# A third bank for the scores of the last eight slots, and three high parts rounded by GpSimd, in an attention block

## The chip, the cores and the metric

The kernel runs on one core of a Trainium2 chip. The metric is device time in microseconds of one execution. TensorE (PE) multiplies into PSUM, VectorE (DVE), ScalarE (ACT) and GpSimd (POOL) work on what it leaves, and SyncE (SP) issues most transfers. GpSimd is used here on SBUF operands alone; the scores lie in PSUM.

## The reference

x has the shape (4, 256, 32, 32): four images, 256 channels, 1024 positions. The reference is a residual self-attention block with four heads of 64 channels:

```
x_n = group_norm(x, 32 groups) * gn_w + gn_b
q, k, v = conv1x1(x_n, wq, bq), conv1x1(x_n, wk, bk), conv1x1(x_n, wv, bv)
q, k, v = to_heads(q), to_heads(k), to_heads(v)          # (b, 4, 1024, 64)
attn = softmax(einsum('bhqd,bhkd->bhqk', q, k) * 64 ** -0.5, axis=-1)
out = einsum('bhqk,bhkd->bhqd', attn, v)
return x + conv1x1(out, wp, bp)
```

## The kernel before, in words

Every fp32 product is made of three fp16 products: each operand is split into a high part (rounded to fp16) and a low part (the difference to fp32, rounded to fp16), and high x high, high x low and low x high are summed in PSUM.

The attention is cut into 128 slots, `TOTAL`, numbered G = 0 to 127, 32 for each image. Four slots make a unit: one head, one half (512) of the queries, and all 1024 keys in four steps of 256. A slot consists of these steps.

- `scores(G)` on TensorE (L718): four products, two for each of two 128-key blocks, into a pair of banks of 1024 fp32 columns. There are two such pairs, `st[0]` and `st[1]`, used by even and odd slots. The second product of each block subtracts a shift, an upper bound made from row maxima, so that the exponential stays in range.
- `exponent(G)` on ScalarE (L954): the exponential of the scores once rounded to fp16 into `p_hi` (L964) and once in fp32 (L969). Even slots write the fp32 copy over the scores in PSUM ("in place"), odd slots write it into one of three SBUF buffers `p32`.
- `p_low(G)`: the difference of the two. Even slots, and the last five slots (`TAIL`), do it on VectorE in two halves (L1086); the other odd slots do it on GpSimd in one piece (L1328).
- `weigh(G)` on TensorE (L747): 24 small products of `p_hi` and `p_lo` with the values, four slots after the scores; the last slots catch up by the table `LAST_WEIGHED`, so that slot 124 weighs slots 120 and 121, and slot 125 weighs 122 and 123.
- After each unit VectorE divides by the denominators, `normalise` (L1089), and the first weighing of the next unit waits for that (L755).

The shift of a unit comes from products of 128 queries with 512 keys of both heads of a pair (`pair_of_maxima`, L686), which VectorE reduces (`row_max`, L1046). Eight such products belong to a pair of units; the last pair is V = 15, for slots 120 to 127. Up to V = 14 two of them are made in every second slot, one in the scores bank `st[1]` that is free just then, and one in the banks `mx`. The eight of V = 15 are made one by one in slots 110 to 117, all in `mx`, so that each waits for the reduction of the one before (L700). After the last, `row_shift` writes the shift, and a transfer puts it into a row of `q_max`, for which slot 120 waits.

The output projection `job("y", ...)` of an image is made in two halves of three products each. For the first 512 positions of the last image, the first halves of the two channel blocks stand in slots 122 and 123 (L805 to L808), in the bank `gen` and in the first bank of `mx`; the second halves follow after slot 127 (L902, L903), ahead of the weighing of slots 126 and 127.

The order of the work is written out by hand for each engine, in loops over the slots. On VectorE a slot runs `p_low(G - 1)` first, then the reductions that `reduced_at(G)` lists, then `normalise` (L1137). On GpSimd slot 117 splits an attention output into high and low part and adds a bias to the residual (`split_output`, `add_bias`), slot 118 does `p_low(117)`, slot 119 the second `add_bias`, slots 120 and 122 do `p_low(119)` and `p_low(121)`, slot 125 splits another output (L1331).

Of the kernel before, what the change touches and what calls it, by code (L numbers as in the profile page):

```python
# [8 lines left out]
ACT = mybir.ActivationFunctionType  # L9
# [3 lines left out]
def attention_block(nc, x, gn_w, gn_b, wq, bq, wk, bk, wv, bv, wp, bp, out):  # L13
    B, C, IH, IW = x.shape
# [7 lines left out]
    HALF = HW // 2  # L22
    QT = HALF // P
    UNITS = HEADS * 2
    SPU = 4
    CPS = NK // SPU
    SLOTS = UNITS * SPU
    TOTAL = B * SLOTS
# [6 lines left out]
    PR = 8  # L35
# [40 lines left out]
    MAX_AFTER = ((), ((0, 0), (0, 1)), (), ((0, 6), (0, 7)), ((1, 0), (1, 1)), ((1, 2), (1, 3)))  # L76
    TAIL = 5

    LAST_WEIGHED = {4: (8, 7), 3: (6, 5), 2: (4,), 1: (3,)}
# [3 lines left out]
    with ctx:  # L83
# [3 lines left out]
        def sem(name):  # L87
            return ctx.enter_context(nc.semaphore(name))
# [73 lines left out]
        first_banks = [st[0][:, 0:512], st[0][:, 512:1024], st[1][:, 0:512], st[1][:, 512:1024], gen, st[1][:, 0:512]]  # L162
        tail_banks = [st[0][:, 0:512], st[0][:, 512:1024], st[1][:, 0:512], st[1][:, 512:1024]]
        last_banks = [gen, mxb[0]]
        row_bank = st[1][:, 512:1024]
# [60 lines left out]
        s_plo_dve = sem("s_plo_dve")  # L226
        s_plo_pool = sem("s_plo_pool")
        s_pv = sem("s_pv")
        s_o32 = sem("s_o32")
# [14 lines left out]
        def wait(eng, s, v):  # L244
            if v > 0:
                eng.wait_ge(s, v)
# [41 lines left out]
        def pair_maxima(G):  # L288

            V, m = divmod(G + PAIR_AHEAD, 2 * SPU)  # L290
            if G in FIRST_PAIRS:
                return [("two", SINGLES // 2, m) for m in FIRST_PAIRS[G]]
            if V == LAST_PAIR:
                return [("two", V, m)]
            if m % 2 or not SINGLES // 2 < V < LAST_PAIR:
                return []
            return [("two", V, m), ("two", V, m + 1)]

        def in_scores_bank(V, m):

            return m in FIRST_IN_SCORES if V == SINGLES // 2 else V < LAST_PAIR and m % 2 == 0

        def maxima_at(G):
            return pair_maxima(G) + single_maxima(G)
# [13 lines left out]
        def one_slot_later(kind, n, m):  # L318

            return kind == "two" and SINGLES // 2 < n < LAST_PAIR and m % 2 == 1  # L320

        def reduced_at(G):

            return [item for item in maxima_at(G) if not one_slot_later(*item)] + \
                   [item for item in pair_maxima(G - 1) if one_slot_later(*item)]

# [65 lines left out]
        def in_place(G):  # L392

            return G % 2 == 0 and G > 0

        def wait_p_lo(eng, G, c=CPS - 1):

            n = sum(lo_on_dve(m) == lo_on_dve(G) for m in range(G))
            wait(eng, *((s_plo_dve, CPS * n + c + 1) if lo_on_dve(G) else (s_plo_pool, n + 1)))
# [23 lines left out]
        def v_rows(tile, i, j):  # L423
            return tile[:, i, 4 * j:4 * j + 4, :, 0:D].rearrange("p c h d -> p (c h) d")

        def p_full(G):

            tile = st[G % 2][:, :] if in_place(G) else p32[:, G // 2 % PB if G else PB - 1, :]
            return tile.rearrange("p (c n) -> p c n", n=HALF)
# [167 lines left out]
        def _(pe):  # L597
# [120 lines left out]
            def scores(G):  # L718
# [12 lines left out]
                if s == 0 and U >= SINGLES and U % 4 == 0:  # L731
                    wait(pe, s_dup_k, 16 * 6 * (U // 4 + 1))
                    wait(pe, s_dup_q[0], 16 * 6 * (U // 4 + 1))
                if G > 1 and not in_place(G - 2):
                    wait(pe, s_exp, G - 1)
                if pair_in_bank(G) is not None:
                    wait(pe, s_mx_free, pair_in_bank(G) + 1)
                for c in range(CPS):
                    if G > 1 and in_place(G - 2):
                        wait_p_lo(pe, G - 2, c)  # L740
                    k = slice((CPS * s + c) * P, (CPS * s + c + 1) * P)
                    dst = st[G % 2][:, c * HALF:(c + 1) * HALF]
                    nc.tensor.matmul(dst, k_both[:, head, k], q_twice[:, head, q], start=True, stop=False)  # L743
                    last = nc.tensor.matmul(dst, k_one[:, head, k], q_max[:, head, q], start=False, stop=True)  # L744
# [40 lines left out]
            def slot(G):  # L785
# [17 lines left out]
                if todo:  # L803
                    job(*todo, only=0 if todo[0] in LONG else None)
                if G in (TOTAL - 6, TOTAL - 5):  # L805
                    i = G - TOTAL + 6
                    wait(pe, s_mx_free, len(in_order))
                    job("y", i, 0, B - 1, last_banks[i], only=0)  # L808

# [92 lines left out]
            job("y", 0, 0, B - 1, last_banks[0], only=1)  # L902
            job("y", 1, 0, B - 1, last_banks[1], only=1)  # L903
            weigh(TOTAL - 2)
# [12 lines left out]
        def _(act):  # L917
# [36 lines left out]
            def exponent(G):  # L954
                scores = st[G % 2][:, :].rearrange("p (c n) -> p c n", n=HALF)
                wait(act, s_st, G + 1)
                wait(act, s_pv, G + 1 - PR)
                if G == TOTAL - 1:
# [4 lines left out]
                    return  # L963
                nc.scalar.activation(p_hi[:, G % PR, :, :], scores, ACT.Exp, scale=SM_SCALE / M_SCALE)  # L964
                if G == 2 * PB - 1:
# [295 lines left out]
        def _(pool):  # L1261
# [64 lines left out]
            def p_low(G):  # L1326
                wait(pool, s_exp, G + 1)
                nc.gpsimd.tensor_tensor(p_lo[:, G % PR, :, :], p_full(G), p_hi[:, G % PR, :, :], ALU.subtract)\  # L1328
                  .then_inc(s_plo_pool, 1)
# [82 lines left out]
```

## Time and profile before

| what | value |
|---|---|
| median of 3 runs | 367.43 us (366.38 to 367.86) |
| the profiled execution | 366.56 us |
| its span, first to last instruction | 364.8 us |
| mean granted TensorE clock | 0.998 |
| TensorE busy | 348.0 us, 95% |
| ScalarE busy | 303.1 us, 83% |
| VectorE, GpSimd busy | 284.0 and 284.2 us, 78% each |

The span holds a prologue of about 16 us, then the 128 slots up to about 358 us, then the last projection and the stores. Slot 110 starts on TensorE at 315.84 us of the span, slot 120 at 338.36 us, slot 127 at 353.23 us. A row of the timeline gives the start, the duration, engine, line and operation, the tile written and the tiles read, their shapes, and in brackets the idle time of the engine before it with what ended it. The weight load of a product (PEld) has its own row.

### The profile page before, as it was taken

The numbers are of one execution on the slowest core, as the hardware profiler recorded it, in microseconds if no ns is written. First come the engines' busy times: TensorE is split into PE (matmuls) and PEld (weight loads), VectorE is DVE, ScalarE is ACT, GpSimd is POOL, SyncE is SP. The second block draws the span as 40 slices with busy tenths as digits, with TensorE's granted clock in tenths as the row PEclk, the third lists the DMA queues.
The fourth block names the chain that finished last, engine by engine and source line by source line (L and its number), as shares of the span: only waits on it lengthen the run. The fifth ranks groups of instructions, "written<-read, shape, count | busy, mean of one in ns | idle before, by whom it ended". The sixth has DMA issues, their size and how long they took to land.

```text
span 364.8 us, 11244 instructions
## 1 busy us (share of the span) xinstructions
PE 348.0 (95%) x4577; PEld 208.6 (57%) x4577; DVE 284.0 (78%) x447; ACT 303.1 (83%) x362; POOL 284.2 (78%) x258
## 2 busy tenths in 40 slices
PE   0899999999999999999999999999999999999996
PEld 0544565655656556655666556565656556655564
DVE  5788899878887787778887777777877787787474
ACT  1748879898877999989878999998889888888982
POOL 5066888699788997998778997998879797967722
PEclk9999999999999999999999999999999999999999
DMA  6055141213743341143553241031552441070113
GB/s 212 19 146 144 45 97 38 30 62 103 135 142 74 80 98 43 24 112 116 124 154 66 60 106 64 10 80 43 117 164 53 94 85 65 2 202 3 31 31 118
DMA packets 38587, 30.92 MB, mean 85 GB/s; under 512 B 23676, under 2 KB 31368, under 8 KB 38536
## 3 DMA queue, kind: packets, MB, share of 16 engines
q1 hardware_dynamic: 37792, 29.15, 32.6%
q10 hardware_dynamic: 744, 1.06, 0.8%
q8 instruction: 37, 0.61, 0.7%
q14 instruction: 14, 0.11, 0.1%
HBM read 9.44 MB, written 4.19 MB: 37 GB/s over the span
## 4 chain that ended last, share of the span: by engine, by line
PE 85%; DVE 8%; ACT 2%; issue 2%; DMA 1%; DVEq 1%; ACTq 0%
PE gen L617 19%; PE st L743 14%; PE st L744 14%; PE pv L766 9%; PE pv L769 8%; PE pv L768 7%; PE st L709 5%; PE mx L709 3%; DVE mx L1053 3%; DVE p_lo L1086 2%; ACT st L969 1%; DVE mx L1049 1%; PE st L617 1%; PE mx L824 1%; DMA xin<-in_x_dram 1%
## 5 line engine op out<-in xcount | busy, mean ns | idle before, releaser
L964 ACT ACTIVATE p_hi<-st 128x1024 f16<-128x1024 f32 x127 | 130.7, 1029 | 40.2 <-PE st L744 38.8
L1328 POOL TENSOR_TENSOR p_lo<-p,p_hi 128x1024 f16<-128x1024 f32 x62 | 132.3, 2133 | 10.4 <-ACT p L969 10.4
L766 PEld LDWEIGHTS pv<-v_hi,p_hi 128*128 128x128 f16 x1024 | 93.4, 97 | 26.7 <-issue 15.0
L766 PE MATMUL pv<-v_hi,p_hi 128*128 128x65 f16 x1024 | 106.4, 195 | 0.3 <-DVE o L1094 0.2
L768 PE MATMUL pv<-v_lo,p_hi 128*128 128x64 f16 x1024 | 105.9, 193 | 0.0
L769 PE MATMUL pv<-v_hi,p_lo 128*128 128x65 f16 x1024 | 105.7, 194 | 0.0
L1086 DVE TENSOR_TENSOR p_lo<-st,p_hi 128x512 f16<-128x512 f32 x126 | 80.8, 683 | 30.0 <-ACT st L969 29.7
L743 PE MATMUL st<-q_twice,k_both 128*128 128x512 f16 x256 | 97.0, 379 | 1.6 <-DVE p_lo L1086 1.2
L768 PEld LDWEIGHTS pv<-v_lo,p_hi 128*128 128x128 f16 x1024 | 93.8, 98 | 6.2
L744 PE MATMUL st<-q_max,k_one 65*128 65x512 f16 x256 | 97.3, 380 | 0.0
L769 PEld LDWEIGHTS pv<-v_hi,p_lo 128*128 128x128 f16 x1024 | 93.9, 97 | 0.0
L1053 DVE TENSOR_REDUCE mx<-st 128x2 f32<-128x1024 f32 x52 | 63.7, 1225 | 25.3 <-PE st L709 25.2
L1053 DVE TENSOR_REDUCE mx<-mx 128x2 f32<-128x1024 f32 x60 | 73.0, 1217 | 1.6 <-PE mx L709 1.6
L969 ACT ACTIVATE st<-st 128x1024 f32<-128x1024 f32 x63 | 65.5, 1040 | 0.0
L969 ACT ACTIVATE p<-st 128x1024 f32<-128x1024 f32 x64 | 65.2, 1018 | 0.0
L743 PEld LDWEIGHTS st<-q_twice,k_both 128*128 128x128 f16 x256 | 25.4, 99 | 26.3 <-issue 7.6
L744 PEld LDWEIGHTS st<-q_max,k_one 65*128 65x128 f16 x256 | 25.0, 97 | 18.4
L459 POOL TENSOR_TENSOR st_lo_k<-e_k,st_hi_k 128x512 f16<-128x512 f32 x16 | 18.5, 1156 | 11.6 <-ACT e_k L939 9.5
L1049 DVE TENSOR_REDUCE mx<-mx 128x1 f32<-128x512 f32 x32 | 20.9, 684 | 4.5 <-PE mx L824 3.0
L1307 POOL TENSOR_TENSOR y<-y,xres 128x512 f32<-128x512 f32 x14 | 17.7, 1270 | 7.6 <-ACT y L948 7.6
L1299 POOL CAST v_hi<-e_v 128x512 f16<-128x512 f32 x16 | 9.8, 614 | 17.0 <-ACT e_v L943 17.0
L617 PE MATMUL gen<-w_hi_v,z_hi 128*128 128x128 f16 x128 | 23.1, 219 | 0.0
(200 smaller groups left out, 558.4 us busy)
## 6 DMA issues: line engine op xcount, KB each, us to landing
q_twice<-st_hi_q SPq DMA_DIRECT2D x64, 64.0 KB, 2.1
xres<-in_x_dram SPq DMA_DIRECT2D x4, 1024.0 KB, 5.2
out_dram<-y SPq DMA_DIRECT2D x13, 256.0 KB, 2.3
xin<-in_x_dram SPq DMA_DIRECT2D x6, 512.0 KB, 4.6
k_both<-st_hi_k SPq DMA_DIRECT2D x16, 128.0 KB, 2.3
k_one<-st_hi_k SPq DMA_DIRECT2D x16, 128.0 KB, 2.6
q_max<-st_lo_q SPq DMA_DIRECT2D x32, 64.0 KB, 2.1
k_both<-st_lo_k SPq DMA_DIRECT2D x16, 128.0 KB, 2.3
```

The lines of the kernel that those rows point to most:

```text
L617: last = nc.tensor.matmul(dst, a, c, start=first and t == 0 and n == 0, stop=t == CT - 1 and n == 2, skip_group_check=True)
L709: last = nc.tensor.matmul(bank[:, h * HALF:(h + 1) * HALF], queries, keys, start=True, stop=True)
L743: nc.tensor.matmul(dst, k_both[:, head, k], q_twice[:, head, q], start=True, stop=False)
L744: last = nc.tensor.matmul(dst, k_one[:, head, k], q_max[:, head, q], start=False, stop=True)
L766: nc.tensor.matmul(pv_v[:, q, :], hi, vh, start=k == 0 and q == 0, stop=False, skip_group_check=True)
L768: nc.tensor.matmul(pv_v[:, q, 0:D], hi, vl, start=False, stop=False, skip_group_check=True)
L769: last = nc.tensor.matmul(pv_v[:, q, :], lo, vh, start=False, stop=k == NK - 1, skip_group_check=True)
L964: nc.scalar.activation(p_hi[:, G % PR, :, :], scores, ACT.Exp, scale=SM_SCALE / M_SCALE)
L969: nc.scalar.activation(p_full(G), scores, ACT.Exp, scale=SM_SCALE / M_SCALE).then_inc(s_exp, 1)
L1053: last = nc.vector.reduce_max(mx8[:, n % 2, :, tile, part], bank[:, :].rearrange("p (h k) -> p h k", h=2), AX.X)
L1086: nc.vector.tensor_tensor(p_lo[:, G % PR, c, :], p_full(G)[:, c, :], p_hi[:, G % PR, c, :], ALU.subtract).then_inc(s_plo_dve, 1)
L1328: nc.gpsimd.tensor_tensor(p_lo[:, G % PR, :, :], p_full(G), p_hi[:, G % PR, :, :], ALU.subtract)\
```

## The change

- The two products m = 0 and 1 of the last pair V = 15 are both made in slot 110, m = 0 in the scores bank `st[1]` and m = 1 in `mx`; slots 111 to 116 make m = 2 to 7, and slot 117 none. VectorE reduces m = 0 in slot 110 and m = 1 in slot 111, ahead of m = 2.
- From slot 120 (`TRIPLE`) on, the scores rotate over three pairs of banks, `mx`, `st[0]`, `st[1]`, and each slot waits for the user of its bank three slots before, not two. Slot 120 waits for the last reduction.
- In slots 117, 119 and 121 (`ONE_EXP`) ScalarE makes the fp32 exponential alone, and GpSimd rounds it to the high part and then subtracts.
- The projection of the second channel block moves as a whole behind slot 127, into `st[1]`; the two tail banks it met there are named anew.

```
+    ONE_EXP = (TOTAL - 11, TOTAL - 9, TOTAL - 7)
+    TRIPLE = TOTAL - 8
...
-        tail_banks = [st[0][:, 0:512], st[0][:, 512:1024], st[1][:, 0:512], st[1][:, 512:1024]]
-        last_banks = [gen, mxb[0]]
+        tail_banks = [st[0][:, 0:512], st[0][:, 512:1024], st[1][:, 512:1024], mxb[0]]
+        last_banks = [gen, st[1][:, 0:512]]
...
             if V == LAST_PAIR:
-                return [("two", V, m)]
+                return [("two", V, n) for n in ((0, 1) if m == 0 else (m + 1,)) if n < 2 * SPU]
...
-            return m in FIRST_IN_SCORES if V == SINGLES // 2 else V < LAST_PAIR and m % 2 == 0
+            return m in FIRST_IN_SCORES if V == SINGLES // 2 else m == 0 or V < LAST_PAIR and m % 2 == 0
...
-            return kind == "two" and SINGLES // 2 < n < LAST_PAIR and m % 2 == 1
+            return kind == "two" and (SINGLES // 2 < n < LAST_PAIR and m % 2 == 1 or (n, m) == (LAST_PAIR, 1))
...
-            return [item for item in maxima_at(G) if not one_slot_later(*item)] + \
-                   [item for item in pair_maxima(G - 1) if one_slot_later(*item)]
+            return [item for item in pair_maxima(G - 1) if one_slot_later(*item)] + \
+                   [item for item in maxima_at(G) if not one_slot_later(*item)]
...
+        def scores_bank(G):
+            return st[G % 2] if G < TRIPLE else (mx, st[0], st[1])[(G - TRIPLE) % 3]
+
+        def bank_user(G):
+            return G - 2 if G < TRIPLE else G - 3
...
-                if G > 1 and not in_place(G - 2):
-                    wait(pe, s_exp, G - 1)
+                if G == TRIPLE:
+                    wait(pe, s_mx_free, len(in_order))
+                elif G > 1 and not in_place(bank_user(G)):
+                    wait(pe, s_exp, bank_user(G) + 1)
...
-                if G in (TOTAL - 6, TOTAL - 5):
-                    i = G - TOTAL + 6
-                    wait(pe, s_mx_free, len(in_order))
-                    job("y", i, 0, B - 1, last_banks[i], only=0)
+                if G == TOTAL - 6:
+                    job("y", 0, 0, B - 1, last_banks[0], only=0)
...
-            job("y", 1, 0, B - 1, last_banks[1], only=1)
+            job("y", 1, 0, B - 1, last_banks[1])
...
-                nc.scalar.activation(p_hi[:, G % PR, :, :], scores, ACT.Exp, scale=SM_SCALE / M_SCALE)
+                if G not in ONE_EXP:
+                    nc.scalar.activation(p_hi[:, G % PR, :, :], scores, ACT.Exp, scale=SM_SCALE / M_SCALE)
...
                 wait(pool, s_exp, G + 1)
+                if G in ONE_EXP:
+                    wait(pool, s_pv, G + 1 - PR)
+                    nc.gpsimd.tensor_copy(p_hi[:, G % PR, :, :], p_full(G)).then_inc(s_phi_pool, 1)
+                    wait(pool, s_phi_pool, ONE_EXP.index(G) + 1)
```

The next two listings are VectorE's order around slots 109 to 112, before and then of the change. `mx8` holds the row maxima; `mx<-mx8` and `shift` close the pair V = 14; the reductions after that are those of V = 15; `p_lo<-st0` is `p_low` of slots 110 and 112.

```order
L1071 TENSOR_REDUCE mx<-mx8 128x8
L1077 TENSOR_SCALAR shift<-mx 128x8
L1053 TENSOR_REDUCE mx8<-mx 128x2
L1086 TENSOR_TENSOR p_lo<-st0,p_hi 128x512 x2
L1053 TENSOR_REDUCE mx8<-mx 128x2
L1093 RECIPROCAL rden<-pv 128x4
L1094 TENSOR_TENSOR o32<-pv,rden 128x4x64
```

```order
L1081 TENSOR_REDUCE mx<-mx8 128x8
L1087 TENSOR_SCALAR shift<-mx 128x8
L1063 TENSOR_REDUCE mx8<-st1 128x2
L1096 TENSOR_TENSOR p_lo<-st0,p_hi 128x512 x2
L1063 TENSOR_REDUCE mx8<-mx 128x2 x2
L1103 RECIPROCAL rden<-pv 128x4
L1104 TENSOR_TENSOR o32<-pv,rden 128x4x64
```

Before, the reduction ahead of `p_lo` is m = 0 and the one behind it m = 1. Now the one ahead is m = 0 out of `st1`, and m = 1 and m = 2, both in `mx`, stand behind it.

The next two listings are GpSimd's order from slot 117 to slot 125, before and then of the change. `o_hi` and `o_lo` are `split_output`, `xres` is `add_bias`, `p_lo` is `p_low` of slots 117, 119 and 121.

```order
L1316 CAST o_hi<-o32 128x512
L1318 TENSOR_TENSOR o_lo<-o32,o_hi 128x512
L1323 TENSOR_SCALAR xres<-xres,bias_y 128x512
L1328 TENSOR_TENSOR p_lo<-p32,p_hi 128x1024
L1323 TENSOR_SCALAR xres<-xres,bias_y 128x512
L1328 TENSOR_TENSOR p_lo<-p32,p_hi 128x1024 x2
L1316 CAST o_hi<-o32 128x512
L1318 TENSOR_TENSOR o_lo<-o32,o_hi 128x512
```

```order
L1326 CAST o_hi<-o32 128x512
L1328 TENSOR_TENSOR o_lo<-o32,o_hi 128x512
L1333 TENSOR_SCALAR xres<-xres,bias_y 128x512
L1340 CAST p_hi<-p32 128x1024
L1342 TENSOR_TENSOR p_lo<-p32,p_hi 128x1024
L1333 TENSOR_SCALAR xres<-xres,bias_y 128x512
L1340 CAST p_hi<-p32 128x1024
L1342 TENSOR_TENSOR p_lo<-p32,p_hi 128x1024
L1340 CAST p_hi<-p32 128x1024
L1342 TENSOR_TENSOR p_lo<-p32,p_hi 128x1024
L1326 CAST o_hi<-o32 128x512
L1328 TENSOR_TENSOR o_lo<-o32,o_hi 128x512
```

Three casts of 1024 columns have come in ahead of three subtractions; nothing else on GpSimd moves. ScalarE's order loses the three `p_hi` passes of these slots.

## Rows read from the trace of the kernel before

**Rows 1.** The page: busy time by engine; shares of the chain that ended last.

```profile
PE 348.0 (95%) x4577; PEld 208.6 (57%) x4577; DVE 284.0 (78%) x447; ACT 303.1 (83%) x362; POOL 284.2 (78%) x258
...
PE 85%; DVE 8%; ACT 2%; issue 2%; DMA 1%; DVEq 1%; ACTq 0%
```

**Rows 2.** Windows: stretch, length, busy PE, PEld, DVE, ACT, POOL, clock, DMA, GB/s.

```profile
334.00:358.00 24.00, 23.22 (x413) 15.90 (x410) 14.99 (x27) 21.86 (x26) 13.49 (x9) 1.00 0.13 24
```

**Rows 3.** Timeline of PE and PEld: what waited, slots 110 to 122.

```profile
317.06 0.41 PE L709 MATMUL mx<-k_both,q_twice 64*128 64x512 f16 x2 [0.18 <-DVE shift L1077]
...
327.03 0.41 PE L709 MATMUL mx<-k_both,q_twice 64*128 64x512 f16 x2 [0.40 <-DVE mx L1053]
...
338.36 0.38 PE L743 MATMUL st<-q_twice,k_both 128*128 128x512 f16 x1 [0.53 <-DVE p_lo L1086]
...
339.46 0.10 PEld L766 LDWEIGHTS pv<-v_hi,p_hi 128*128 128x128 f16 x1 [0.48 <-DVE o L1094]
...
342.24 0.39 PE L743 MATMUL st<-q_twice,k_both 128*128 128x512 f16 x1 [0.26 <-DVE p_lo L1086]
...
342.83 0.10 PEld L743 LDWEIGHTS st<-q_twice,k_both 128*128 128x128 f16 x1 [0.48 <-DVE p_lo L1086]
```

**Rows 4.** Timeline of slot 111: scores and maximum on PE, then DVE.

```profile
318.81 0.38 PE L743 MATMUL st<-q_twice,k_both 128*128 128x512 f16 x1
...
319.77 0.41 PE L709 MATMUL mx<-k_both,q_twice 64*128 64x512 f16 x2
...
319.05 1.29 DVE L1086 TENSOR_TENSOR p_lo<-st,p_hi 128x512 f16<-128x512 f32 x2 [0.32 <-ACT st L969]
320.26 1.22 DVE L1053 TENSOR_REDUCE mx<-mx 128x2 f32<-128x1024 f32 x1
```

**Rows 5.** Timeline of PE: first score product of slots 117, 118, 119.

```profile
332.45 0.38 PE L743 MATMUL st<-q_twice,k_both 128*128 128x512 f16 x1
...
334.49 0.38 PE L743 MATMUL st<-q_twice,k_both 128*128 128x512 f16 x1
...
336.08 0.38 PE L743 MATMUL st<-q_twice,k_both 128*128 128x512 f16 x1
```

**Rows 6.** Timeline of PE: slot 123's projection half, then slot 124's first score product.

```profile
346.26 0.38 PE L617 MATMUL mx<-oT_hi,w_hi_p 128*128 128x512 f16 x1
...
346.91 0.38 PE L743 MATMUL st<-q_twice,k_both 128*128 128x512 f16 x1
```

**Rows 7.** Timeline of DVE: p_low of slot 118, then the division of its unit.

```profile
337.53 1.29 DVE L1086 TENSOR_TENSOR p_lo<-st,p_hi 128x512 f16<-128x512 f32 x2 [1.31 <-ACT st L969]
...
338.98 0.42 DVE L1094 TENSOR_TENSOR o<-pv,rden 128x256 f32<-128x256 f32 x1
```

**Rows 8.** Timeline of POOL: p_low of 115, 117, 121, second add_bias, last split.

```profile
331.20 2.13 POOL L1328 TENSOR_TENSOR p_lo<-p,p_hi 128x1024 f16<-128x1024 f32 x1 [2.42 <-ACT p L969]
...
336.65 2.14 POOL L1328 TENSOR_TENSOR p_lo<-p,p_hi 128x1024 f16<-128x1024 f32 x1
338.77 1.57 POOL L1323 TENSOR_SCALAR xres<-xres,bias_y 128x512 f32<-128x512 f32 x1
...
343.38 2.13 POOL L1328 TENSOR_TENSOR p_lo<-p,p_hi 128x1024 f16<-128x1024 f32 x1 [0.94 <-ACT p L969]
...
348.08 1.49 POOL L1318 TENSOR_TENSOR o_lo<-o,o_hi 128x512 f16<-128x512 f32 x1
```

**Rows 9.** Groups of POOL by shape: busy us, mean ns of one.

```profile
L1328 POOL TENSOR_TENSOR p_lo<-p,p_hi 128x1024 f16<-128x1024 f32 x62 | 132.3, 2133 | 10.4 <-ACT p L969 10.4
L459 POOL TENSOR_TENSOR st_lo_k<-e_k,st_hi_k 128x512 f16<-128x512 f32 x16 | 18.5, 1156 | 11.6 <-ACT e_k L939 9.5
...
L1316 POOL CAST o_hi<-o 128x512 f16<-128x512 f32 x15 | 9.2, 613 | 1.9 <-DVE o L1094 1.9
```

**Rows 10.** Timeline of DVE: p_low of slots 123 and 125, out of SBUF.

```profile
347.70 2.42 DVE L1086 TENSOR_TENSOR p_lo<-p,p_hi 128x512 f16<-128x512 f32 x2 [0.37 <-ACT p L969]
...
352.33 1.28 DVE L1086 TENSOR_TENSOR p_lo<-p,p_hi 128x512 f16<-128x512 f32 x2
```

More of the change, by code:

```diff
@@ L227, in attention_block @@
         s_plo_pool = sem("s_plo_pool")
+        s_phi_pool = sem("s_phi_pool")
         s_pv = sem("s_pv")
@@ L424, in v_rows @@
             return tile[:, i, 4 * j:4 * j + 4, :, 0:D].rearrange("p c h d -> p (c h) d")
+        def scores_bank(G):
+            return st[G % 2] if G < TRIPLE else (mx, st[0], st[1])[(G - TRIPLE) % 3]
+        def bank_user(G):
+            return G - 2 if G < TRIPLE else G - 3
         def p_full(G):
-            tile = st[G % 2][:, :] if in_place(G) else p32[:, G // 2 % PB if G else PB - 1, :]
+            tile = scores_bank(G)[:, :] if in_place(G) else p32[:, G // 2 % PB if G else PB - 1, :]
             return tile.rearrange("p (c n) -> p c n", n=HALF)
@@ L738, in scores @@
                 for c in range(CPS):
-                    if G > 1 and in_place(G - 2):
-                        wait_p_lo(pe, G - 2, c)
+                    if G > 1 and G != TRIPLE and in_place(bank_user(G)):
+                        wait_p_lo(pe, bank_user(G), c)
                     k = slice((CPS * s + c) * P, (CPS * s + c + 1) * P)
-                    dst = st[G % 2][:, c * HALF:(c + 1) * HALF]
+                    dst = scores_bank(G)[:, c * HALF:(c + 1) * HALF]
                     nc.tensor.matmul(dst, k_both[:, head, k], q_twice[:, head, q], start=True, stop=False)
@@ L954, in exponent @@
             def exponent(G):
-                scores = st[G % 2][:, :].rearrange("p (c n) -> p c n", n=HALF)
+                scores = scores_bank(G)[:, :].rearrange("p (c n) -> p c n", n=HALF)
                 wait(act, s_st, G + 1)
```

## The prediction

> **What bounds the kernel now.** I read the busy times first, then the chain that ended last: TensorE is busy 348.0 of 364.8 us, and 85% of the chain is its own work [rows 1]. So a gain must be TensorE idle time that goes, and any new idle time there is lost. The change touches slots 110 to 127 only, so I read that stretch next. From 334 to 358 us the granted clock is 1.00, the 2.4 GHz level, and I reckon with that level after the change too. TensorE is busy 23.22 of 24 us there, ScalarE 21.86, VectorE 14.99, GpSimd 13.49 [rows 2]: ScalarE has 2 us of air, GpSimd over 10. Last, the waits of TensorE one by one [rows 3]: before slot 120 for p_low(118), 0.53 us, and in the same slot for the division of the unit before; in slot 122 for p_low(120); earlier 0.40 us in slot 114 for a reduction. These are what a third bank and a shorter ScalarE could give back.
>
> Sizes used below. Three products of 512 columns take 346.91 - 346.26 = 0.65 us [rows 6], so four score products take 0.87. A slot of scores and one weighing is 336.08 - 334.49 = 1.59, so a weighing is 0.72; a slot with a maximum is 334.49 - 332.45 = 2.04, so the maximum is 0.45 [rows 5].
>
> **The change part by part,** as the delay of TensorE against the same event before.
>
> 1. Slot 111, +1.75. The maximum of slot 111 is now m = 2 in mx, and must wait until VectorE has reduced m = 1 out of the same banks. That reduction stands behind p_low(110), which waits for ScalarE's exponential of slot 110. Before, m = 1 was reduced at exactly this place of VectorE's order: p_low(110) from 319.05, the reduction from 320.26 to 321.48, while TensorE had issued its product at 319.77 [rows 4]. Now TensorE can issue only at 321.5: 321.5 - 319.77 = 1.75. Behind it on TensorE are the second half of a value projection, weighing 107 and all later slots. The second maximum of slot 110 costs at most its 0.45, and ends in this wait, so it adds nothing; VectorE has room for it, since m = 0 no longer waits for the shift of V = 14 (0.18 [rows 3]).
> 2. Slots 112 to 116, +-0. Scores, exponentials, subtractions and reductions all move by the same 1.75 and keep their order, so the 0.40 wait in slot 114 returns. Delay still 1.75.
> 3. Slot 117, -0.45 for the maximum that is gone. But scores 118 need p_low(116), which VectorE does just behind the last reduction and the shift: between 0 and 0.45 of the gain is lost there, I take 0.2. Delay 1.5.
> 4. Slot 120, +-0. Scores 120 go to mx and no longer wait for p_low(118); the shift's transfer is two microseconds earlier relative to them. But weighing 116, next on TensorE, waits for the division, and that stands on VectorE behind the same p_low(118), from 337.53, with the division's end at 338.98 + 0.42 = 339.40 [rows 7]; TensorE took it at 339.46 [rows 3]. From scores 118 at 334.49 to there is 4.97; TensorE's own work on the way is 1.59 + 1.59 + 0.87 = 4.05 [rows 5, 6]. So 0.9 of idle time stays, in one place instead of two. ScalarE's missing pass of slot 117 doesn't shorten this chain: it runs ahead of scores 118, not behind. Delay still 1.5.
> 5. Slot 122, -0.6. From 339.46 to 342.24 are 2.78 us with work of 0.72 + 0.87 + 0.72 = 2.31: 0.47 is lost, and the second half starts at 342.83, not at 342.24 + 0.43 = 342.67: another 0.16 [rows 3]. The third bank removes both, since scores 122 wait for slot 119 only. Delay 0.9.
> 6. The first projection half of slot 123 moves behind slot 127: -0.65 here [rows 6], +0.65 at the end. Before, weighing 121 (the second of slot 124) started at 346.91 + 0.87 + 0.72 = 348.50. TensorE alone would now reach it at 348.50 + 0.9 - 0.65 = 348.75.
> 7. GpSimd. p_low(115) started when its exponential ended, at 331.20, and GpSimd then ran without a pause to p_low(117) at 336.65; p_low(121) waited 0.94 for ScalarE and was done at 345.5, 3 us before it was needed [rows 8]. The new cast of 1024 columns is in no row. The nearest is the cast of 512, 0.613; the subtraction goes from 1.156 at 512 to 2.133 at 1024 [rows 9], that is 0.18 fixed, so 2 x 0.613 - 0.18 = 1.05 for the cast. From below it is bounded by 0.61 (no dearer than half its size), from above by 2.13 (as dear as the subtraction, which reads two operands); I take 1.05, the nearest row doubled, and 0.1 for the wait between cast and subtraction. From 331.20 + 1.75 = 332.95 the same 5.45 us lead to 338.40; then three times 1.15 + 2.13, and 1.57 for the bias in between: 338.40 + 9.84 + 1.57 = 349.8. The waits for p_low(117) and (119) cost TensorE about nothing (341.7 against 342.5; 346.6 against 346.5), that for p_low(121) costs a microsecond.
> 8. Contention. Where VectorE's p_low(123), out of SBUF, ran beside GpSimd, its pair took 2.42 against 1.28 for that of slot 125 [rows 10], and GpSimd's subtraction of 512 columns beside it 1.49 [rows 8] against 1.16 [rows 9]: both slowed. Now p_low(123), from about 348.6, meets p_low(121). I add the 0.3 of that row: 350.1. The Trainium skill ("SBUF — State Buffer", section "SBUF: two separate sides") says that a VectorE instruction with two SBUF inputs and a GpSimd instruction take a shared pair of ports as a lock, and that the later one fully blocks. By that rule p_low(121), which starts first, would lose nothing, and the sum would be 0.3 smaller. The trace agrees only in part: VectorE loses 1.1 us there, but GpSimd does too.
>
> Sum: weighing 121 at 350.1 against 348.50 is +1.6. From there to the end TensorE does what it did before, which was without a real pause, plus the moved 0.65: +2.25. A wait of at most 0.2 for the last subtraction, which TensorE would now miss, goes off: I take +2.2 us. The three passes taken from ScalarE, with air of 2 us, are worth nothing by this. The profiled execution took 366.56 us, 1.8 more than its span; 366.56 + 2.2 = 368.8. It lay 0.9 under the median of the runs, 367.43, so the median of the changed kernel comes to 369.6.
>
> **The rivals.**
> A. GpSimd is on time: a cast near its lower bound, 0.61, takes 3 x 0.44 = 1.3 off step 7, and weighing 121 starts when TensorE comes, at 348.75. Then +0.25 + 0.65 = +0.9 and 368.3. For it: 0.61 is known for half the size. Against it: the subtraction nearly doubles with its size. It shows as no wait of TensorE for GpSimd.
> B. GpSimd is dearer: a cast of 1.6, midway to the upper bound, or a lock that holds each of them: 3 x 0.55 = 1.65 more, +3.9 and 371.3. For it: GpSimd's chain has no air from 331 on. Against it: no cast in the trace is near that.
> C. ScalarE paces the tail (faster). If exponentials, not TensorE, set the pace from slot 118, the three passes of some 0.92 each are worth up to 2.76, against the 1.5 that is left after step 3: -1.3 and 366.1. It decides from scores 118 on, provided GpSimd delivers p_low(121) by 347. For it: ScalarE is busy 21.86 of 24 us [rows 2]. Against it: p_low on VectorE waits for ScalarE, but ScalarE itself starts when the scores end, and step 7 has GpSimd late by then.
>
> **How the numbers follow.** My forecast 60%, own range 368.8 to 370.5; A 20%, B 13%, C 7%. About 0.5% (1.84 us) is what a measurement of this kernel can tell from no change: slower means above 369.3, faster below 365.6. Two thirds of the forecast and B are slower: 0.40 + 0.13, and with a little of A 0.55. Half of C, at most, is faster: 0.04. The rest, 0.41, is within. The upper bound of the cast (2.13) would give 372.8, which I hold for unlikely; the range goes from just under A, 367.9, to just under B, 371.0.
>
> **What would show it.** Right: TensorE's maximum of slot 111 starts over 1.2 us later relative to its scores, with a wait for VectorE's mx; at weighing 116 a wait of 0.6 to 1.1 for the division; none for p_low at scores 120 and 122; a GpSimd cast of 1.0 to 1.2 us; a wait of about a microsecond for p_low(121) ahead of weighing 121; GpSimd without a pause from p_low(115) to p_low(121). Wrong: no wait in slot 111 (then step 1 falls, and with it most of the sum), a cast under 0.8 or over 1.4, or exponentials that follow each other without a gap while TensorE waits for them.

## The result and the profile after

The changed kernel takes 369.47 us (median of 6 executions, 368.55 to 370.33); the kernel before, on the same chip, 366.90 (6 executions, 366.15 to 367.86). The ratio is 1.0072 [1.0056, 1.0088]: slower by 2.57 us, where +2.2 was forecast and 369.6 named. The profiled execution took 369.86 us with a span of 368.1, against 366.56 and 364.8 before, so the two traces differ by 3.30. That is what the ledger below has to explain.

Of the changed kernel the page, busy time by engine and the shares of the chain that ended last, against [rows 1]:

```profile
PE 349.3 (95%) x4577; PEld 209.3 (57%) x4577; DVE 284.2 (77%) x447; ACT 300.6 (82%) x359; POOL 287.4 (78%) x261
...
PE 81%; DVE 6%; POOL 5%; issue 3%; DMA 2%; ACT 2%; DVEq 1%; POOLq 0%; ACTq 0%
```

ScalarE has lost three passes and 2.5 us, GpSimd has gained three casts and 3.2 us. TensorE executes the same 4577 products but is busy for 1.3 us longer, so something slowed it while it worked. GpSimd, absent from the chain of before, now holds 5% of it.

The timeline of TensorE in the changed kernel (start, duration, what it waited for), from the scores of slot 111 to the last projection; the places are those of [rows 3] and [rows 4]:

```profile
318.99 0.38 PE L754 MATMUL st<-q_twice,k_both 128*128 128x512 f16 x1
...
321.75 0.40 PE L718 MATMUL mx<-k_both,q_twice 64*128 64x512 f16 x2 [1.73 <-DVE mx L1063]
...
324.31 0.62 PE L754 MATMUL st<-q_twice,k_both 128*128 128x512 f16 x1
...
326.07 0.41 PE L718 MATMUL mx<-k_both,q_twice 64*128 64x512 f16 x2
...
330.62 0.41 PE L718 MATMUL mx<-k_both,q_twice 64*128 64x512 f16 x2 [0.39 <-DVE mx L1063]
...
338.24 0.10 PEld L754 LDWEIGHTS st<-q_twice,k_both 128*128 128x128 f16 x1 [0.49 <-DVE p_lo L1096]
...
342.80 0.20 PE L777 MATMUL pv<-v_hi,p_hi 128*128 128x65 f16 x1 [0.76 <-DVE o L1104]
...
348.26 0.10 PEld L777 LDWEIGHTS pv<-v_hi,p_hi 128*128 128x128 f16 x1 [0.34 <-POOL p_lo L1342]
...
350.11 0.10 PEld L777 LDWEIGHTS pv<-v_hi,p_hi 128*128 128x128 f16 x1 [0.57 <-DVE o L1104]
...
351.46 0.20 PE L777 MATMUL pv<-v_hi,p_hi 128*128 128x65 f16 x1 [0.45 <-POOL p_lo L1342]
...
358.15 0.39 PE L626 MATMUL gen<-oT_hi,w_hi_p 128*128 128x512 f16 x1 [0.20 <-DMA oT_lo<-o_lo]
```

The maximum of slot 111 waits 1.73 us for VectorE's reduction (mx), where before it started without a wait. Later, weighing 116 waits 0.76 for the division (o), and weighing 121 waits 0.45 for GpSimd's subtraction. The weight load of weighing 119 waits 0.34 for GpSimd too, but its first product, at 348.27, is not late by it; that of weighing 120 waits 0.57 for the division. The waits for p_low at scores 120 and 122 [rows 3] are gone. The score product of slot 112 at 324.31 takes 0.62 us instead of 0.38.

That last number leads to the windows (length, busy PE, PEld, DVE, ACT, POOL with their instructions, granted clock, DMA share, GB/s). The changed kernel, from the wait of slot 111 on:

```profile
320.00:322.00 2.00, 0.27 (x3) 0.11 (x2) 1.70 (x2) 1.94 (x2) 0.27 (x1) 1.00 0.58 99
322.00:324.00 2.00, 2.00 (x33) 1.91 (x32) 1.23 (x1) 0.60 (x1) 0.11 (x1) 0.63 0.51 180
324.00:326.00 2.00, 2.00 (x14) 0.76 (x11) 0.61 (x2) 0.00 (x0) 1.92 (x3) 0.52 1.08 281
326.00:328.00 2.00, 2.00 (x31) 1.16 (x30) 1.23 (x1) 1.82 (x2) 1.79 (x1) 1.00 0.83 303
```

The kernel before in two of the same windows:

```profile
322.00:324.00 2.00, 2.00 (x32) 1.11 (x31) 1.47 (x2) 1.72 (x3) 1.55 (x2) 1.00 0.80 241
324.00:326.00 2.00, 2.00 (x31) 1.15 (x30) 1.60 (x4) 1.89 (x3) 2.00 (x2) 1.00 1.02 274
```

Behind the wait the granted clock falls to 0.63 and 0.52, near the 1.2 GHz level, and TensorE gets through 14 products from 324 to 326 instead of 31, though not of the same mix of shapes. From 326 on it is back at 2.4 GHz. "Busy 2.00 of 2.00" looks alike in both: only the clock column and the counts tell the two apart.

**The ledger.** Delay against the same event before, without the 0.18 us by which scores 111 already lagged (318.99 against 318.81):

| event | after | before | net delay | step |
|---|---|---|---|---|
| maximum of slot 111 | 321.75 | 319.77 | +1.80 | +1.80: wait for the reduction |
| maximum of slot 112 | 326.07 | 322.48 | +3.41 | +1.61: low granted clock |
| weighing 116 | 342.79 | 339.46 | +3.15 | -0.26 |
| weighing 118 | 346.01 | 343.28 | +2.55 | -0.60: no waits for p_low in slot 122 |
| scores 124 | 349.01 | 346.91 | +1.92 | -0.63: projection half moved away |
| weighing 120 | 350.12 | 347.78 | +2.16 | +0.24: wait for the division |
| weighing 121 | 351.46 | 348.50 | +2.78 | +0.62: wait for GpSimd |
| last division | 361.77 | 357.87 | +3.72 | +0.94: 0.65 projection, 0.37 wait for oT_lo, -0.08 a wait that is gone |
| end of the span | | | +3.12 | -0.60: last division to the end 6.33 us, not 6.93 |

The steps go from start to start. A wait is larger there than in its row, because the row counts only from the end of the product before: 0.62 against 0.45 at weighing 121, 0.37 against 0.20 for oT_lo.

With the 0.18 that makes 3.30. Two terms, both in slots 111 and 112, are 3.41 of it; all that comes later adds up to -0.29.

GpSimd's chain in the changed kernel, from p_low(115) to the last split, which answers to [rows 8]:

```profile
334.79 2.12 POOL L1342 TENSOR_TENSOR p_lo<-p,p_hi 128x1024 f16<-128x1024 f32 x1 [2.43 <-ACT p L979]
...
340.22 1.04 POOL L1340 CAST p_hi<-p 128x1024 f16<-128x1024 f32 x1
341.34 2.13 POOL L1342 TENSOR_TENSOR p_lo<-p,p_hi 128x1024 f16<-128x1024 f32 x1
...
349.27 2.13 POOL L1342 TENSOR_TENSOR p_lo<-p,p_hi 128x1024 f16<-128x1024 f32 x1
351.35 1.08 POOL L1326 CAST o_hi<-o 128x512 f16<-128x512 f32 x1
352.50 1.48 POOL L1328 TENSOR_TENSOR o_lo<-o,o_hi 128x512 f16<-128x512 f32 x1
```

From 334.79 it runs without a pause to 351.40, the end of p_low(121), and weighing 121 starts at 351.46. So GpSimd hands its own late start on to weighing 121, whatever TensorE gains on the way. VectorE's work at the two places of the sum, in the changed kernel ([rows 4], [rows 7] and [rows 10] have it before):

```profile
319.28 1.29 DVE L1096 TENSOR_TENSOR p_lo<-st,p_hi 128x512 f16<-128x512 f32 x2 [0.57 <-ACT st L979]
320.48 1.22 DVE L1063 TENSOR_REDUCE mx<-mx 128x2 f32<-128x1024 f32 x1
...
340.86 1.29 DVE L1096 TENSOR_TENSOR p_lo<-st,p_hi 128x512 f16<-128x512 f32 x2 [2.67 <-ACT st L979]
...
342.31 0.42 DVE L1104 TENSOR_TENSOR o<-pv,rden 128x256 f32<-128x256 f32 x1
...
350.43 1.52 DVE L1096 TENSOR_TENSOR p_lo<-p,p_hi 128x512 f16<-128x512 f32 x1 [0.37 <-ACT p L979]
351.88 1.09 DVE L1096 TENSOR_TENSOR p_lo<-p,p_hi 128x512 f16<-128x512 f32 x1
```

The reduction that slot 111 waits for ends at 321.70, and TensorE starts at 321.75. p_low(118) begins 2.67 us after VectorE's last work, and the division still stands behind it.

### The profile page after: what moved, and what is told of

It reads as the page before. It is cut to its first block, busy times and chain, and to the rows that moved or that the text cites. A ratio compares the mean times of both kernels' runs of the same rounds, so it can differ in the third digit from the quotient of the medians.

```text
span 368.1 us, 11247 instructions
## 1 busy us (share of the span) xinstructions
PE 349.3 (95%) x4577; PEld 209.3 (57%) x4577; DVE 284.2 (77%) x447; ACT 300.6 (82%) x359; POOL 287.4 (78%) x261
## 4 chain that ended last, share of the span: by engine, by line
PE 81%; DVE 6%; POOL 5%; issue 3%; DMA 2%; ACT 2%; DVEq 1%; POOLq 0%; ACTq 0%
PE gen L626 19%; PE st L754 13%; PE st L755 13%; PE pv L777 8%; PE pv L780 7%; PE pv L779 7%; PE st L718 5%; PE mx L718 3%; POOL p_lo L1342 2%; DVE mx L1063 2%; PE st L626 1%; DVE p_lo L1096 1%; DMA oT_lo<-o_lo 1%; DVE mx L1059 1%; DMA xin<-in_x_dram 1%
## 5 line engine op out<-in xcount | busy, mean ns | idle before, releaser
L974 ACT ACTIVATE p_hi<-st 128x1024 f16<-128x1024 f32 x121 | 124.6, 1029 | 42.5 <-PE st L755 41.1
L1096 DVE TENSOR_TENSOR p_lo<-st,p_hi 128x512 f16<-128x512 f32 x122 | 78.3, 683 | 28.3 <-ACT st L979 28.0
L754 PE MATMUL st<-q_twice,k_both 128*128 128x512 f16 x250 | 95.3, 381 | 0.8 <-DVE p_lo L1096 0.4
L755 PE MATMUL st<-q_max,k_one 65*128 65x512 f16 x250 | 95.4, 382 | 0.0
L1063 DVE TENSOR_REDUCE mx<-st 128x2 f32<-128x1024 f32 x53 | 65.0, 1226 | 25.6 <-PE st L718 25.4
L1063 DVE TENSOR_REDUCE mx<-mx 128x2 f32<-128x1024 f32 x59 | 71.8, 1218 | 2.3 <-PE mx L718 2.3
L979 ACT ACTIVATE p<-st 128x1024 f32<-128x1024 f32 x63 | 64.1, 1018 | 0.9 <-PE st L755 0.9
L979 ACT ACTIVATE st<-st 128x1024 f32<-128x1024 f32 x61 | 63.5, 1041 | 0.0
L626 PE MATMUL gen<-w_hi_v,z_lo 128*128 128x128 f16 x128 | 23.3, 220 | 0.0
```

Source lines behind the costliest of these rows:

```text
L626: last = nc.tensor.matmul(dst, a, c, start=first and t == 0 and n == 0, stop=t == CT - 1 and n == 2, skip_group_check=True)
L979: nc.scalar.activation(p_full(G), scores, ACT.Exp, scale=SM_SCALE / M_SCALE).then_inc(s_exp, 1)
L1063: last = nc.vector.reduce_max(mx8[:, n % 2, :, tile, part], bank[:, :].rearrange("p (h k) -> p h k", h=2), AX.X)
L1096: nc.vector.tensor_tensor(p_lo[:, G % PR, c, :], p_full(G)[:, c, :], p_hi[:, G % PR, c, :], ALU.subtract).then_inc(s_plo_dve, 1)
```

## The experiments

The theory was that all of the loss is in slot 111: the wait, and the low clock behind it. The runs undo it, separate its two terms, and do it alone. The first four ran beside 19 executions of the kernel before (366.39 us, 365.38 to 367.67), the last four beside 27 (366.77, 365.51 to 368.01).

**e1_reduce_m1_early.** The changed kernel, but m = 1 of the last pair is reduced in its own slot, not one later:

```
-            return kind == "two" and (SINGLES // 2 < n < LAST_PAIR and m % 2 == 1 or (n, m) == (LAST_PAIR, 1))
+            return kind == "two" and SINGLES // 2 < n < LAST_PAIR and m % 2 == 1
```

> The changed kernel with one edit: VectorE reduces m = 1 in slot 110, right behind m = 0 and ahead of p_low(110), so TensorE finds mx free in slot 111. Theory 1 (the wait in slot 111, 1.75 us, and the stretch of granted clock 0.5 to 0.6 behind it, 1.6 us, make the loss): both go, what is left is GpSimd's late p_low(121) and the moved projection, 367.2 to 367.6 us, 0.3 to 0.7 over the kernel before; granted clock 1.00 from 322 to 326 us. Theory 2 (GpSimd's three casts make the loss, and the wait in slot 111 would be taken up later): 368.8 or more, with a wait for p_low(121) that has grown to 2 us.

Measured: 366.23 us (365.42 to 366.54), ratio to before 0.9996 [0.9984, 1.0008]. The whole loss is gone; the time is even below the 367.2 to 367.6 of the first theory, and the 368.8 of the second is out. That theory had counted the waits for GpSimd and the moved projection as loss; by the ledger all that follows slot 112 comes to -0.29. In slot 111 the products wait for nothing any more. The first row is the weight load of that maximum:

```profile
320.39 0.11 PEld L718 LDWEIGHTS mx<-k_both,q_twice 64*128 64x128 f16 x2 [0.43 <-DVE mx L1063]
...
339.81 0.20 PE L777 MATMUL pv<-v_hi,p_hi 128*128 128x65 f16 x1 [0.75 <-DVE o L1104]
...
348.49 0.20 PE L777 MATMUL pv<-v_hi,p_hi 128*128 128x65 f16 x1 [0.46 <-POOL p_lo L1342]
```

It idles 0.43 us, as that of a maximum of the changed kernel does at 332.67, where no product waits; in the changed kernel it idled 2.22 us in slot 111. The two later waits, for the division and for GpSimd, are as in the changed kernel (0.76 and 0.45): they are not what made it slower.

**e2_busy_in_wait.** The changed kernel with its wait, but in slot 111 TensorE computes 30 products into columns that nothing reads, ahead of the maxima:

```
+                if G == 111:
+                    for _ in range(30):
+                        nc.tensor.matmul(pv[:, 384:512], ident_16[:, :], ident_16[:, :], start=False, stop=True,
+                                         skip_group_check=True)
```

> The changed kernel with 30 more products of 128 columns on TensorE ahead of the maximum of slot 111, into columns of the pv bank that nothing reads: the wait for VectorE stays, but TensorE isn't idle in it. Theory 1 with the clock as a consequence of the idle time: the maximum starts where it did, the granted clock stays at 1.00, and 1.6 us come back, about 368.0. Theory 3 (the low clock has nothing to do with the idle time): unchanged, 369.5, with the same low clock behind the wait. Theory 2: at most 0.5 less than 369.5.

Measured: 367.63 us (366.96 to 368.22, 8 executions), ratio 1.0037 [1.0019, 1.0055]. The products fill the wait (TensorE is idle for 0.05 us from 320 to 322), and behind it the clock remains at 1.00:

```profile
320.00:322.00 2.00, 1.95 (x33) 1.73 (x31) 1.88 (x3) 1.75 (x2) 0.45 (x1) 1.00 0.84 117
322.00:324.00 2.00, 2.00 (x40) 1.65 (x41) 1.35 (x2) 0.79 (x2) 0.18 (x1) 1.00 0.45 155
```

More work made the kernel faster. By the medians the idle time's price splits so: this run is 367.63 - 366.23 = 1.4 us above e1, which is the wait alone; from 1.0037 to the 1.0072 of the changed kernel, 0.0035 x 366.4 = 1.3 us, is the clock. The traces have 1.80 and 1.61 for the two. These medians mix clocks: six of e1's twelve executions and two of e2's eight have a mean clock of 0.995, among them both profiled ones, whose low stretch lies in the prologue and not behind slot 111. Among the executions at 1.000 the medians are 365.78 and 367.46, so the wait alone comes to 1.7, close to the trace. The third theory falls.

**e3_two_passes.** The changed kernel with ScalarE's two passes and no cast on GpSimd in the three slots:

```
-    ONE_EXP = (TOTAL - 11, TOTAL - 9, TOTAL - 7)
+    ONE_EXP = ()
```

> The changed kernel with ONE_EXP empty: ScalarE makes both passes in slots 117, 119 and 121 again, and GpSimd only subtracts. Theory 1: GpSimd's chain is worth the waits of TensorE for it, 0.34 + 0.45, of which half comes back as waits for the divisions: 369.1. Theory 2: 1.5 to 2.6 us come back, 367 to 368.

Measured: 368.13 us (367.01 to 370.00, 6 executions), ratio 1.0066 [1.0040, 1.0092], not told apart from the whole change. So the casts are not the loss either. The spread is wide, and the profiled execution, the fastest, shows one reason: it has the same wait in slot 111, and no low clock behind it.

```profile
321.21 0.41 PE L718 MATMUL mx<-k_both,q_twice 64*128 64x512 f16 x2 [1.73 <-DVE mx L1063]
```

```profile
322.00:324.00 2.00, 2.00 (x38) 1.33 (x34) 1.49 (x3) 0.60 (x1) 0.83 (x2) 1.00 0.97 300
```

Its mean clock was 1.000 and its time 367.01; the other five had 0.991 to 0.995 and 367.7 to 370.0. So the same idle time is followed by the low clock in the profiled executions of the changed kernel and of e4 (below), and not in this one. Where the other five had theirs, a mean does not tell.

**e4_maxima_alone.** The kernel before with the maxima's four edits only (two banks, two passes, the projection where it was):

```
-                return [("two", V, m)]
+                return [("two", V, n) for n in ((0, 1) if m == 0 else (m + 1,)) if n < 2 * SPU]
...
-            return m in FIRST_IN_SCORES if V == SINGLES // 2 else V < LAST_PAIR and m % 2 == 0
+            return m in FIRST_IN_SCORES if V == SINGLES // 2 else m == 0 or V < LAST_PAIR and m % 2 == 0
...
-            return kind == "two" and SINGLES // 2 < n < LAST_PAIR and m % 2 == 1
+            return kind == "two" and (SINGLES // 2 < n < LAST_PAIR and m % 2 == 1 or (n, m) == (LAST_PAIR, 1))
...
-            return [item for item in maxima_at(G) if not one_slot_later(*item)] + \
-                   [item for item in pair_maxima(G - 1) if one_slot_later(*item)]
+            return [item for item in pair_maxima(G - 1) if one_slot_later(*item)] + \
+                   [item for item in maxima_at(G) if not one_slot_later(*item)]
```

> The kernel before with the new order of the maxima of the last pair alone (two in slot 110, m = 1 reduced in slot 111), without the third bank, the one-pass exponentials or the moved projection. Theory 1: the wait in slot 111 and the low clock come with it, less what the later waits give back: 369.5 to 370.2, as slow as the whole change or slower. Theory 2: 367, as before.

Measured: 368.90 us (368.54 to 369.07, 6 executions, mean clock 0.994 to 0.995 in all), ratio 1.0072 [1.0054, 1.0090]: the whole loss, to the digit, from the maxima alone. The wait and then the window behind it:

```profile
321.44 0.41 PE L709 MATMUL mx<-k_both,q_twice 64*128 64x512 f16 x2 [1.73 <-DVE mx L1053]
...
341.45 0.38 PE L743 MATMUL st<-q_twice,k_both 128*128 128x512 f16 x1 [0.59 <-DVE p_lo L1086]
```

```profile
322.00:324.00 2.00, 2.00 (x37) 2.00 (x35) 1.12 (x1) 0.60 (x1) 0.48 (x1) 0.57 0.79 259
```

With two banks, scores 120 again wait for p_low(118), 0.59 us, and the time is no worse than with three.

**e5_old_maxima.** The complement: the changed kernel with those four edits undone (the first stands here, the other three are those of e4 read backwards), so with the third bank, the casts and the moved projection.

```
-                return [("two", V, n) for n in ((0, 1) if m == 0 else (m + 1,)) if n < 2 * SPU]
+                return [("two", V, m)]
...
```

> The changed kernel with the maxima of the last pair in the order of the kernel before (one in each of slots 110 to 117, all in mx); third bank, one-pass exponentials and moved projection stay. If the whole loss lies in the maxima's order, this is as fast as the kernel before: 366.2 to 366.9. If the third bank needs the maxima a slot earlier (slot 120 then waits for the shift or for mx): 367 or more, with that wait ahead of scores 120.

Measured: 366.54 us (365.52 to 366.97, 12 executions), ratio 0.9993 [0.9976, 1.0010]. So these three parts together are worth nothing. Where the waits went:

```profile
337.77 0.39 PE L754 MATMUL mx<-q_twice,k_both 128*128 128x512 f16 x1 [0.34 <-DMA q_max<-shift]
...
347.48 0.20 PE L777 MATMUL pv<-v_hi,p_hi 128*128 128x65 f16 x1 [0.19 <-POOL p_lo L1342]
```

Scores 120 no longer wait for p_low, but for the shift, which is only just there, and weighing 121 waits for GpSimd.

**e6_early_two_passes.** e1 and `ONE_EXP = ()`: the maxima one slot earlier without the wait, the third bank, no casts.

```
-    ONE_EXP = (TOTAL - 11, TOTAL - 9, TOTAL - 7)
+    ONE_EXP = ()
```

> m = 1 reduced in slot 110, third bank, and both passes on ScalarE (ONE_EXP empty). Against the run with early reduction and one-pass exponentials (366.23): the waits for GpSimd (0.36 and 0.46) go, but the wait for the division ahead of weighing 120 grows and ScalarE gets 2.8 us more, so I expect 366.0 to 366.3. If GpSimd's rounding is what holds the third bank back: 365.2 or less.

Measured: 365.75 us (365.11 to 366.68, 12 executions), ratio 0.9973 [0.9958, 0.9989]: faster than before by 1 us, inside the 0.5% that the prediction drew, and between the two expectations (366.0 and 365.2). Against e1 (0.9996) the casts cost some 0.8 us, though the two intervals overlap. Among executions with a mean clock of 0.999 or more, each against the kernel before beside it, the two figures are 0.7 and 0.5. No weighing waits for GpSimd any more; the two waits of the weighings are for VectorE:

```profile
338.86 0.20 PE L777 MATMUL pv<-v_hi,p_hi 128*128 128x65 f16 x1 [0.82 <-DVE o L1104]
...
346.42 0.20 PE L777 MATMUL pv<-v_hi,p_hi 128*128 128x65 f16 x1 [0.32 <-DVE o L1104]
```

Both wait for the division of the unit, which VectorE does behind p_low of the slot before. The same p_low, then the division, on VectorE:

```profile
336.93 1.29 DVE L1096 TENSOR_TENSOR p_lo<-st,p_hi 128x512 f16<-128x512 f32 x2 [2.73 <-ACT st L979]
...
338.38 0.42 DVE L1104 TENSOR_TENSOR o<-pv,rden 128x256 f32<-128x256 f32 x1
```

The last product of the sums that the division reads starts on TensorE at

```profile
336.98 0.20 PE L780 MATMUL pv<-v_hi,p_lo 128*128 128x65 f16 x1
```

In e7 below, the reciprocal starts 0.23 us after that product (337.04 and 336.81). Here it could by that have gone at about 337.2, but it starts at 338.13, behind p_low, which began at 336.93: some 0.9 us are the order in VectorE's queue. TensorE needs the division first.

**e7_divide_first.** e6, and in slots 119 and 123 VectorE divides ahead of p_low, not behind it:

```
+    DIVIDE_FIRST = (TOTAL - 9, TOTAL - 5)
...
+                if G in DIVIDE_FIRST:
+                    normalise(G // SPU - 1)
...
-                    if old % SPU == SPU - 1:
+                    if old % SPU == SPU - 1 and G not in DIVIDE_FIRST:
```

> As the run before it, and VectorE divides first in slots 119 and 123, ahead of p_low(118) and p_low(122). If the third bank is worth nothing because weighings 116 and 120 wait for a division that stands behind p_low (0.75 and 0.55 us), both waits go and 1.0 to 1.3 us come out: 364.9 to 365.3. If ScalarE or VectorE paces this stretch instead, the waits move to the scores and nothing comes out: 366.1.

Measured: 364.45 us (363.96 to 365.74, 7 executions), ratio 0.9943 [0.9921, 0.9966], 2.3 us under the kernel before beside it: faster than both kernels, the changed one standing at 1.0072, and lower than the 364.9 expected at best, since e6 itself lay under 366. Among executions with a mean clock of 0.999 or more it is 1.7 us under the kernel before and 1.0 under e6 (364.39 against 365.39), as forecast for the two waits. On VectorE the reciprocal now starts as soon as the sums are there, and p_low is next:

```profile
337.04 0.18 DVE L1104 RECIPROCAL rden<-pv 128x4 f32<-128x4 f32 x1 [3.02 <-PE pv L781]
...
337.64 1.28 DVE L1097 TENSOR_TENSOR p_lo<-st,p_hi 128x512 f16<-128x512 f32 x2
```

The weight loads of TensorE beside it, weighing 116 and then the next scores:

```profile
337.78 0.10 PEld L778 LDWEIGHTS pv<-v_hi,p_hi 128*128 128x128 f16 x1 [0.40 <-DVE o L1105]
...
338.98 0.10 PEld L755 LDWEIGHTS st<-q_twice,k_both 128*128 128x128 f16 x1 [0.34 <-DVE p_lo L1097]
```

Weighing 116 waits 0.40 on its weights, where e6 had 1.31, and p_low, which is later by 0.7, costs 0.34 on the weights of the scores that need it. TensorE's busy time in the window of [rows 2], here and then in the changed kernel (the same times of the span; the changed kernel is two or three slots behind there):

```profile
334.00:358.00 24.00, 23.88 (x406) 16.48 (x406) 13.71 (x28) 21.43 (x27) 14.24 (x10) 1.00 0.20 37
```

```profile
334.00:358.00 24.00, 22.50 (x389) 14.75 (x387) 14.75 (x27) 19.60 (x22) 18.78 (x13) 1.00 0.27 24
```

0.12 us idle instead of 1.50, and 0.78 before [rows 2]. ScalarE is busier than in the changed kernel, GpSimd has its air back, and it is TensorE's column that decides. Dividing first with only two banks was not run, so how much of the gain needs the third bank is not shown.

**e8_divide_first_one.** e7 with the cast on GpSimd in one slot, `ONE_EXP = (TOTAL - 7,)`:

```
-    ONE_EXP = ()
+    ONE_EXP = (TOTAL - 7,)
```

> As the run before it, with the one-pass exponential in slot 121 alone. GpSimd then has one cast and air for it: 364.7 to 365.2, the fastest of all by a tenth or two, if ScalarE's passes of slots 120 to 123 are the next wait; else the same as the run before it.

Measured: 364.76 us (363.64 to 365.58, 9 executions), ratio 0.9938 [0.9918, 0.9958], not told apart from e7. One cast fits into GpSimd's air and relieves nothing that TensorE waits for.

## Why the prediction was right, and where it was not

The time came out (369.47 against 369.6), and so did slower as the likeliest side. The mechanism named first was the one that counts: e4 shows that the maxima's order is the whole loss, e1 that without the late reduction there is none. But the sum was right partly because errors cancelled.

- **Step 1** holds: +1.80 measured, 1.75 forecast, with the wait for mx that it names.
- **"I reckon with that level after the change too"** (the granted clock) failed. After 1.73 us of idle time, in which TensorE ran 3 products in 2 us, the clock went to 0.63 and 0.52, which cost 1.61 us in the trace and about 1.3 by the medians of e2. The prediction read the clock only where the change ends, 334 to 358, and not in the place where it put the new idle time.
- **Steps 2 to 4** hold: the wait in slot 114 is back (0.39), and from slot 112 to weighing 116 the delay falls by 0.26, where 1.75 - 1.5 = 0.25 was forecast. Step 3 has its row at 338.24: the second half of scores 118 waits for p_low(116), and of the 0.44 that the missing maximum gives, 0.17 is lost, where 0.2 was taken. The third bank does take the wait for p_low away, and weighing 116 waits for the division, 0.76 by its row and 0.92 from start to start (0.9 forecast). e7 shows the step's reason from the other side: moved ahead of p_low, the division no longer costs that, and the time falls.
- **Steps 5 and 6** hold: the wait for p_low at scores 122 is gone, which takes 0.60 off (0.6 forecast), the projection half takes another 0.63 off (0.65 forecast), and it is paid back at the end. The +0.94 there has a wait that the sum did not have, 0.37 for the transfer of oT_lo: GpSimd makes that low part behind p_low(121), so the transfer is issued at 354.01 instead of 349.60. The "at most 0.2 for the last subtraction" that the sum took off is another wait, 0.08 us ahead of weighing 127 before, and it is gone.
- **Step 7** holds in kind and nearly in size. The cast took 1.036 us (mean of three), estimated 1.05. From p_low(115) to the end of p_low(121) GpSimd took 16.61 us, against 16.85 forecast without the contention. The wait at weighing 121 came to 0.62 us where 1.35 (350.1 against 348.75) was forecast, because the 0.30 of step 8 and 0.24 of the chain did not come, and because weighing 120 waited 0.24 for its division, which the sum had left out; the 0.05 that remains is the step from GpSimd's end to TensorE's start.
- **Step 8** failed: the 0.3 us did not come. p_low(121) started first, at 349.27, and took 2.13 us, its usual time. The two subtractions of VectorE beside it took 1.52 and 1.09 us, where one alone takes 0.68, and GpSimd's next cast and subtraction of 512 columns, which began while these were running, 1.08 and 1.48 instead of 0.61 and 1.16. The Trainium skill ("SBUF — State Buffer", section "SBUF: two separate sides") says that whichever of the two starts first keeps the shared ports and the other blocks. These rows agree with that: VectorE's first subtraction started with 0.97 us of p_low(121) left and lost 0.84, and the three that follow lost 0.47, 0.41 and 0.32 where 0.60, 0.55 and 0.47 were left of the one before. Each lost all that was left but 0.13 to 0.15 us. The kernel before, whose row the prediction took as agreeing "only in part", shows the same once VectorE's pair is read one by one:

```profile
347.70 0.85 DVE L1086 TENSOR_TENSOR p_lo<-p,p_hi 128x512 f16<-128x512 f32 x1 [0.37 <-ACT p L969]
...
348.47 1.65 DVE L1086 TENSOR_TENSOR p_lo<-p,p_hi 128x512 f16<-128x512 f32 x1
```

GpSimd's subtraction of 1.49 us [rows 8] started at 348.08, inside the first of these. It was the later one and lost 0.33 of 0.47; the second, starting inside it, lost 0.97 of 1.10. The prediction carried that 0.3 over to p_low(121), which was the earlier one.

- **From profile to median.** The forecast put the median 0.87 above the profiled execution, as it stood before (366.56 and 367.43). The changed kernel's median lies 0.39 below its profiled execution (369.47 and 369.86).

By the traces the change costs 3.30 us where the sum said 2.25. The 1.05 between them are 0.18 and 0.05 ahead of and in step 1, +1.61 for the clock, +0.29 at the end of TensorE's work (the wait for oT_lo, less the one that is gone), against -0.47 between weighings 116 and 121 (0.30 of contention, most of the rest in GpSimd's chain) and -0.60 after it, where the stores landed sooner; the 0.01 left is in steps 2 to 4. The conversion to medians then takes 0.87 + 0.39 = 1.26 back. So the mechanism and the side were right, and the range held what was missed; that the point came within 0.2 us was luck.

Of the rivals, A (GpSimd on time) is out, since weighing 121 waits for it; B (GpSimd dearer) is out with a cast of 1.04; C (ScalarE paces) is out, since without the wait the passes taken from ScalarE bring nothing (e1), and e6, which gives them back, is no slower. The row of the single pass of slot 121 in the changed kernel says it too:

```profile
344.61 1.02 ACT L979 ACTIVATE p<-st 128x1024 f32<-128x1024 f32 x1 [0.59 <-PE st L755]
```

ScalarE waits there for TensorE's scores, not the other way.

What stays open: why the same 1.73 us is followed by the low clock in the profiled executions of the changed kernel and of e4, and not in that of e3. The mean clocks (0.990 to 0.995 in all 12 executions of those two, 1.000 in one of e3's six) fit, but a mean clock does not show where the low stretch lies; only a profiled execution does. Of the kernel before, 4 of 19 executions had a mean of 0.993 to 0.995.

## What to carry to other kernels

A product that is made earlier gains nothing while the reduction that frees its bank stays where it was queued: look at the order on the engine that frees the bank, and at what the queue's head waits for, not at its busy share. One more bank helps little while the next instruction in line waits for the same chain; here the division behind p_low was that chain, and moving two divisions gave what the third bank and the casts had not (with the third bank in place; without it this was not run). When a change puts idle time on TensorE, price the clock behind it as well as the idle time itself, and bound it by rows at either level.

## What the runs showed of the hardware

- In two of three profiled executions an idle stretch of 1.73 us was followed by some 3 us of low granted clock (0.52 to 0.63 over windows of 2 us), which cost 1.3 (medians) to 1.6 us (trace), nearly as much as the wait; in the third the clock stayed at 1.00. With useless products in the wait it stayed at 1.00 there in the profile of e2.
- The low clock is not bound to one place. A profiled execution of e1, with no such wait in slot 111, had it in the prologue, where TensorE ran 5 and 6 products in 2 us. The profile of the kernel before, with 6 and 8 products there, was granted 1.00:

```profile
18.00:20.00 2.00, 1.63 (x5) 0.33 (x4) 2.00 (x4) 0.30 (x1) 2.00 (x2) 0.78 0.71 211
20.00:22.00 2.00, 2.00 (x6) 0.74 (x6) 0.71 (x2) 0.49 (x1) 0.15 (x1) 0.50 0.33 117
```

- Its six executions with a mean clock of 1.000 took 365.42 to 366.15 us, the six with 0.995 took 366.31 to 366.54: a difference of a few tenths between two kernels means nothing before their clocks are compared.
- GpSimd's cast from fp32 to f16 went from 0.613 us at 512 columns [rows 9] to 1.036 at 1024, half the price of the subtraction that reads two operands (2.13).
- Where a subtraction of VectorE with both inputs in SBUF and an instruction of GpSimd overlapped, the later one came out longer by what was left of the earlier, less 0.13 to 0.15 us: six times in two traces (step 8).
